# Attention products as three 16-bit products, with another order of the stages in a step

## The reference, cut to what matters

```python
qkv = silu(hidden_states @ qkv_w.T)            # q, k, v of 32 heads x 64
# blocks of 32 tokens, a running state per head:
aw = einsum('bhid,bhjd->bhij', qi, ki) * dd    # dd: decay by distance, 0 above the diagonal
intra = einsum('bhij,bhjd->bhid', aw, vi)
inter = einsum('bhid,bhde->bhie', qi * qd, state)
new_state = state * bd + einsum('bhsd,bhse->bhde', ki * kd, vi)
attn = rmsnorm(intra + inter) * norm_w
gate = sigmoid(hidden_states @ gate_w.T)
x = layernorm(hidden_states + gate * attn @ out_w.T)
x = layernorm(x + moe(x))                      # grouped top-6 of 64 experts, and a shared one
```

## Time and profile before

| | |
|---|---|
| median of 3 timed runs | 1415.9 us (1414.46 to 1415.93) |
| the profiled execution | 1412.41 us, span 1410.4 us |
| mean granted TensorE clock | 0.981 of full speed |
| busy: TensorE, VectorE, ScalarE, GpSimd | 1345.9, 894.6, 671.2, 366.5 us |

### The profile page before, as it was taken

How to read it: one execution, slowest core, us unless ns; L and a number is a source line. 1 busy time by engine, 2 the same in 40 slices (tenths; PEclk the granted TensorE clock), 3 DMA queues, 4 the chain that set the end, 5 groups by cost and what they waited for, 6 DMA issues and landing times.

```text
span 1410.4 us, 36483 instructions
## 1 busy us (share of the span) xinstructions
PE 1345.9 (95%) x13995; PEld 1096.4 (78%) x13995; DVE 894.6 (63%) x2468; ACT 671.2 (48%) x1290; POOL 366.5 (26%) x422
## 2 busy tenths in 40 slices
PE   7999999999999999999999999999999999989960
PEld 5888888888888888888888888888888888865530
DVE  7856576666667575756576666667575756553337
ACT  8644454545454544445454545444444445433314
POOL 0212121212121122212121212121122222337754
PEclk9999999999999999999999999999999999999985
DMA  8500000000000000000000000000000000779957
GB/s 314 194 9 10 25 15 24 15 24 15 24 15 24 7 17 22 7 26 13 24 15 24 15 24 15 24 15 24 7 14 25 7 24 15 228 247 248 239 111 303
DMA packets 52962, 86.38 MB, mean 61 GB/s; under 512 B 6752, under 2 KB 32192, under 8 KB 52032
## 3 DMA queue, kind: packets, MB, share of 16 engines
q1 hardware_dynamic: 41728, 70.33, 14.7%
q0 software_dynamic: 5632, 8.26, 3.4%
q10 hardware_dynamic: 5568, 7.34, 1.5%
HBM read 60.08 MB, written 25.83 MB: 61 GB/s over the span
## 4 chain that ended last, share of the span: by engine, by line
PE 89%; DMA 4%; DVE 3%; issue 1%; POOL 1%; ACT 1%; SPq 0%; ACTq 0%; DVEq 0%; POOLq 0%
PE pA L467 25%; PE pB L467 23%; PE pC L543 13%; PE pO L557 12%; PE pS L529 10%; DMA sums<-sb_stage,sb_sidx 2%; PE pC L467 1%; PE pS L718 1%; DMA sb_W<-sums 1%; PE pC L577 1%; PE pB L701 1%; POOL sums L1292 0%; PE pS L701 0%; DVE sb_W L921 0%; DMA sb_stage<-gather_rows,sb_gidx 0%
## 5 line engine op out<-in xcount | busy, mean ns | idle before, releaser
L467 PE MATMUL pB<-sb_xh,sb_W 128*128 (+1 forms) x2048 | 349.9, 273 | 0.0
L1244 POOL TENSOR_TENSOR sb_fold<-sb_sq 128x256 f32<-128x256 f32 x128 | 111.5, 871 | 893.9 <-ACT sb_sq L801 893.9
L467 PE MATMUL pB<-sb_xl,sb_W 128*128 (+1 forms) x1024 | 279.3, 273 | 0.0
L467 PEld LDWEIGHTS pB<-sb_xh,sb_W 128*128 128x128 f16 x2048 | 200.5, 98 | 23.8 <-issue 0.2
L799 ACT ACTIVATE sb_yh<-sb_y 128x512 f16<-128x512 f32 x128 | 80.6, 630 | 286.4 <-DVE sb_y L937 286.4
L543 PE MATMUL pC<-sb_S,sb_v 128*64 128x256 f32 (+1 forms) x2048 | 194.7, 332 | 0.0
L945 DVE TENSOR_TENSOR sb_ql<-sb_q,sb_qh 128x512 f16<-128x512 f32 x128 | 88.0, 687 | 167.7 <-ACT sb_qh L775 164.3
L774 ACT ACTIVATE sb_q<-pA 128x512 f32<-128x512 f32 x128 | 76.4, 597 | 223.2 <-PE pA L467 223.1
L467 PE MATMUL pA<-sb_xh,sb_W 128*128 (+1 forms) x1024 | 175.9, 274 | 5.7 <-DVE sb_W L921 5.7
L467 PE MATMUL pA<-sb_W,sb_xh 128*128 128x256 f16 x1024 | 177.0, 275 | 2.1 <-ACT sb_qh L775 2.1
L557 PE MATMUL pO<-sb_Wo,sb_yh 128*128 128x256 f16 x1024 | 174.7, 273 | 1.0 <-DVE sb_yl L941 1.0
(11 more groups left out here) (210 smaller groups left out, 2315.5 us busy)
## 6 DMA issues: line engine op xcount, KB each, us to landing
sb_stage<-wprep SPq DMA_DIRECT2D x7, 1280.0 KB, 6.6
sb_W<-sums SPq DMA_DIRECT2D x16, 512.0 KB, 11.1
sb_W<-w_experts SPq DMA_DIRECT2D x16, 384.0 KB, 5.4
gather_rows<-sb_xr SPq DMA_DIRECT2D x16, 320.0 KB, 2.3
sb_D<-w_experts SPq DMA_DIRECT2D x12, 384.0 KB, 4.4
sb_xs<-xT SPq DMA_DIRECT2D x17, 256.0 KB, 2.9
sb_D<-decay SPq DMA_DIRECT2D x8, 512.0 KB, 7.6
sb_xn<-x SPq DMA_DIRECT2D x16, 256.0 KB, 3.0
```

The costliest lines, as they stand in the source:

```text
L467: last = nc.tensor.matmul(dst, a, m, start=(i == 0), stop=(i == len(terms) - 1), **kw)
L1244: nc.gpsimd.tensor_tensor(fold[:, :], sq[:, 0:T], sq[:, T:2 * T], ALU.add).then_inc(s_fold, 1)
```

## The change

1. **Attention in 16 bit.** v and S get an upper part (vh, Sh) and a lower part (vl, Sl) in 16 bit. `attention` makes three products (vh Sh, vl Sh, vh Sl) where it had one in float32. The upper parts are made on ScalarE (`high_v`, `high_S`), the lower part of v on GpSimd (`low_v`), the lower part of S for the first 256 columns of each head on GpSimd and for the other 128 on VectorE (`low_S`).
2. **Decay product** in two instructions over all four heads, first part then second.
3. **Order.** On TensorE: project_q, scores(g-1), project_k, attention(g-2), project_v, output(g-3), project_gate. The small pieces move: sum of squares to q=2, transposes to the end of q=3, router to q=4, counts to q=6, all but the transposes right behind `scores`. On VectorE `decayed` comes first, then `gate`, low_q, low_k, low_S, low_y, with the routing spread between. On ScalarE the squares come before the upper part of y.
4. **Space and semaphores.** wsh and triu32 lie in xr until they are used; the first three units lie in the weights' staging buffer; the decay tables use two semaphores in place of eight, so the load of a table waits for the one two before it.
5. **Tail.** The units are shared out differently over the tail's steps.

```diff
-        v32 = [sb(f"v32{i}", [P, NT, QH * HD]) for i in range(2)]
+        v32 = sb("v32", [P, NT, QH * HD])
+        vh = [sb(f"vh{i}", [P, NT, QH * HD], F16) for i in range(2)]
+        vl = [sb(f"vl{i}", [P, NT, QH * HD], F16) for i in range(2)]
+        Sh = sb("Sh", [P, QH, T + P], F16)
+        Sl = sb("Sl", [P, QH, T + P], F16)
...
-        TAIL = ["g0 g1", "d0 g2 d1 g3 d2 g4", "", "d3 d4", "g5 g6 d5 g7 d6", "", "g8 d7 g9 d8 g10 d9", "", "g11 d10 d11"]
+        TAIL = ["g0 g1", "d0 g2", "d1 g3 d2 g4", "", "g5 g6 d5 g7 d6", "g8 d7 g9 d8 g10 d9", "", "", "g11 d10 d11"]
+        BETWEEN = "d3 d4"
+        HALVES = [(0, T), (T, T + P)]
...
             def load_decays(Q):
-                sp.dma_start(D[:, Q, :], decay[Q]).then_inc(s_decay[Q], 16)
+                wait(sp, s_decay[Q % 2], 16 * (Q // 2))
+                sp.dma_start(D[:, Q, :], decay[Q]).then_inc(s_decay[Q % 2], 16)
...
             def attention(q, h):
-                pe.wait_ge(s_Sm, 2 * h + 2)
-                pe.wait_ge(s_ve, h + 1)
+                pe.wait_ge(s_Sl0, h + 1)
+                pe.wait_ge(s_Sl1, h + 1)
+                pe.wait_ge(s_vl, h + 1)
                 wait(pe, s_sq, h)
+                wait(pe, s_y, h)
                 i = q % 2
+                products = [(vh[i], Sh), (vl[i], Sh), (vh[i], Sl)]
                 for u in range(2):
-                    for t in range(NT):
-                        for e in range(2):
...
+                    for t, (a, z_) in enumerate(HALVES):
+                        for n, (v, s) in enumerate(products):
+                            for e in range(2):
+                                head = 2 * u + e
+                                last = nc.tensor.matmul(pC[64 * e:64 * e + 64, u * T + t * P:(u + 1) * T],
+                                                        v[:, t, head * HD:(head + 1) * HD], s[:, head, a:z_],
+                                                        start=(t == 0 and n == 0), stop=(t == NT - 1 and n == len(products) - 1))
                 last.then_inc(s_C, 1)
...
                 if has(g):
                     project_q(b, q, g)
-                    project_k(b, q, g)
                 if has(g - 1):
                     scores((q - 1) % NQ, g - 1)
+                if behind(b):
+                    if q == 2:
+                        sum_squares(b, g - 2)
+                    if q == 4:
+                        router(b)
+                    if q == 6:
+                        count(b, g - 2)
+                if has(g):
+                    project_k(b, q, g)
...
                 if has(g - 2):
                     bank_of_attention(b, q)
                     attention((q - 2) % NQ, g - 2)
...
                 if has(g):
                     project_v(b, q, g)
+                if has(g - 3) and not (tail and q == 1):
+                    output(b, (q - 3) % NQ, g - 3)
+                if has(g):
                     project_gate(b, q, g)
-                if has(g - 2):
-                    output(b, (q - 2) % NQ, g - 2)
-                if behind(b):
-                    piece(b, q, g - 1)
...
+                if behind(b) and q == 3:
+                    transpose_rows(b, g - 1)
...
             def act_v(q, g):
                 act.wait_ge(s_v, g + 1)
+                wait(act, s_vl, g)
+                nc.scalar.activation(v32[:, :, :].rearrange("p t n -> p (t n)"), pA[:, :], ACT.Silu,
+                                     scale=1 / W_SCALE).then_inc(s_ve, 1)
+
+            def high_v(q, g):
+                act.wait_ge(s_ve, g + 1)
                 wait(act, s_C, g - 1)
...
+                nc.scalar.activation(vh[q % 2][:, :, :], v32[:, :, :], ACT.Copy).then_inc(s_vh, 1)
+
+            def high_S(h, i):
+                act.wait_ge(s_Sm, 2 * h + i + 1)
+                wait(act, s_C, h)
+                a, z_ = HALVES[i]
+                nc.scalar.activation(Sh[:, :, a:z_], S[:, :, a:z_], ACT.Copy).then_inc(s_Sh, 1)
...
-            def decayed(b, q, h, u):
...
+            def decayed(b, q, h):
+                dve.wait_ge(s_S, 2 * h + 2)
...
+                d = D[:, q, :].rearrange("p (h n) -> p h n", h=QH)
+                wait(dve, s_Sl0, h)
+                nc.vector.tensor_tensor(S[:, :, 0:T], pS[:, :, 0:T], d, ALU.mult).then_inc(s_Sm, 1)
+                wait(dve, s_Sl1, h)
+                nc.vector.tensor_tensor(S[:, :, T:T + P], pS[:, :, T:T + P], d[:, :, 0:P], ALU.mult).then_inc(s_Sm, 1)
+
+            def low_S(h):
+                dve.wait_ge(s_Sh, 2 * h + 2)
+                a, z_ = HALVES[1]
+                nc.vector.tensor_tensor(Sl[:, :, a:z_], S[:, :, a:z_], Sh[:, :, a:z_], ALU.subtract).then_inc(s_Sl1, 1)
...
+            def low_v(q, g):
+                pool.wait_ge(s_vh, g + 1)
+                wait(pool, s_C, g - 1)
+                nc.gpsimd.tensor_tensor(vl[q % 2][:, :, :], v32[:, :, :], vh[q % 2][:, :, :], ALU.subtract).then_inc(s_vl, 1)
+
+            def low_S(h):
+                pool.wait_ge(s_Sh, 2 * h + 1)
+                a, z_ = HALVES[0]
+                nc.gpsimd.tensor_tensor(Sl[:, :, a:z_], S[:, :, a:z_], Sh[:, :, a:z_], ALU.subtract).then_inc(s_Sl0, 1)
```

More of the change, by code:

```diff
@@ new lines, in router, with count @@
+            def router(b):
+                pe.wait_ge(s_x1T, b)
+                for t in range(NT):
+                    last = group(pC[:, t * EXP:(t + 1) * EXP],
+                                 [(x1T[:, c, t * P:(t + 1) * P], wr[:, c, :]) for c in range(NC)])
+                last.then_inc(s_r, 1)
+            def count(b, attended):
+                bank_free(attended)
+                pe.wait_ge(s_mask, b)
+                nc.tensor.matmul(pC[0:EXP, 0:T], mask[:, 0, :], triu[:, 0:T], start=True, stop=False)
+                nc.tensor.matmul(pC[0:EXP, P:T], mask[:, 1, :], triu[:, 0:P], start=False, stop=True).then_inc(s_cum, 1)
@@ L846, in step @@
                     split_weights(q + 1, (0, 1))
+                if behind(b) and q == 4 and not tail:
+                    evacuate_router(b)
                 if has(g):
@@ L967, in residual @@
             def residual(b):
-                chain = Chain(dve, s_ln1, LN1_LINKS * (b - 1), s_dve_passed)
                 dve.wait_ge(s_D, 8 * b)
@@ L1106, in step @@
                     split_weights(q + 1)
+                if has(g - 1):
+                    decayed(b, (q - 1) % NQ, g - 1)
+                if behind(b):
+                    if q == 3:
+                        statistics(b)
+                    if q == 4:
+                        route_scores(b)
+                    if q == 5:
+                        route_experts(b)
+                if has(g - 2):
+                    gate((q - 2) % NQ, g - 2)
                 if has(g):
@@ L1110, in step @@
                     split_weights(q + 1, (0, 1))
+                if behind(b) and q == 3:
+                    normed(b)
                 if has(g):
@@ L1258, in step @@
                 last_b = isinstance(b, int) and b == SEQS
-                if last_b and q == 2:
-                    unit_product(2)
+                if has(g - 1):
+                    low_v((q - 1) % NQ, g - 1)
                 if behind(b) and q == 2:
@@ L1265, in step @@
                         unit_product(3)
+                if behind(b) and q == 3:
                     pool.wait_ge(s_var, b)
                     nc.gpsimd.tensor_tensor(rstd2[:, 0:NT], vv[:, 0:NT], mhalf[:, 0:NT], ALU.pow).then_inc(s_rstd2, 1)
+                if has(g - 1):
+                    low_S(g - 1)
                 if has(g - 2):
```

194 lines of the change are left out of this document (100 added, 94 removed).

## The result

| | before | after |
|---|---|---|
| median | 1415.2 us (1413.3 to 1415.9, 4 runs) | 1493.4 us (1491.4 to 1496.9, 4 runs) |
| span of the profiled execution | 1410.4 | 1493.8 |
| first projection of sequence 1 (read at ScalarE's evacuation of q) | 80.9 | 97.2 |
| mean length of a sequence in the loop | 75.66 | 79.27 |
| from the same evacuation in the last step (127) to the end | 203.9 | 219.0 |

The changed kernel is 5.6% slower (ratio 1.056, 95% interval 1.053 to 1.058), where 1396 was forecast. The table divides the 83 us between the two spans: 16 before sequence 1, 52 from there to step 127, 15 behind it.

The account below looks back on a forecast made before the run. TensorE's own work was taken to bound the loop. Attention -32, the q=2 wait +7.5 and the first sequence +5 gave -19.5 us, median 1415.9 to 1396, range 1380 to 1418.

Parts of the forecast that it names:

- TensorE's part: Attention block in each step: 16-bit products and four change-overs take 1.27 us against 1.54; 0.25 saved, 128 x 0.25 = 32 us.
- GpSimd's durations: GpSimd's added subtractions in each step: low_v 1.15 us, low_S of 1024 elements 2.2; sum about 5.0 of 8.95 us.
- rival (B): GpSimd and the shared access become the bound; gain gone at about 2.55 us for low_S, near 1471 at 3.0; chance 0.17.
- Who would be late: The four engines' orders laid side by side in a step: three tight places, only one priced, 7.5 us in all.
- the sum of squares at q=2: TensorE's sum_squares right behind scores waits for GpSimd's fold and acc: 0.5 us a sequence, 15 x 0.5 = 7.5 us.
- (2): At q=4 VectorE does low_x1 and route_scores before gate and low_k; kl just in time for next scores; taken as nothing.
- (3): At q=3 transpose_rows needs statistics, rstd2 and normed inside the step; about 0.6 us to spare; taken as nothing.
- 7.4 us of exclusive time: VectorE's two-SBUF-input instructions (2.4 us) plus GpSimd's work (5.0), which exclude each other, in a step of 8.95 us.
- The first sequence: Steps 2 to 6, where ScalarE and VectorE also split weights, take 9.2 to 10.5 instead of 8.95: 5 us lost.
- The tail: From the end of the last projection to the sum of squares, 13.5 us before: no change taken, within 1 us.
- rival (A): Nothing is late, GpSimd's instructions slip between VectorE's: -32 to -36 us, 1380 to 1384; chance 0.16.

Follow-up runs that it names:

- the order alone, freed: Changed kernel with attention left in float32 and only the new order kept, two buffers for multiplied scores, TensorE's program written out: 1436.5 us, ratio 1.013 to 1.016.

## Why the prediction was wrong

**TensorE's part** was right for the products. A plain step is 8.97 against the forecast 8.95. The attention products start 0.11 us apart at 256 columns and 0.05 to 0.06 at 128, as they were priced:

```profile
642.74 0.28 PE L559 MATMUL pC<-sb_Sl,sb_vh 128*64 128x256 f16 x2
642.85 0.22 PE L559 MATMUL pC<-sb_Sh,sb_vh 128*64 128x128 f16 x2
642.90 0.22 PE L559 MATMUL pC<-sb_Sh,sb_vl 128*64 128x128 f16 x2
```

With the subtractions left out and no fetches, a sequence takes 73.86: 1.80 less, where 8 x 0.25 = 2.0 was the term. The change-over was 0.11, not 0.09. That run's 1396 is the forecast number by chance: it leaves out work, it has the later unit loads, and it has not the stalls that the forecast held.

**TensorE's part left out the loop's turn.** I counted products and not instructions. The body grew from 1697 to 1828 and began elsewhere, and each turn waits 1.7 to 2.3 us for instructions, at times with a slower clock behind it. The runs put 41 us on it where nothing else is late, 10 in the changed kernel as it stands. No row of before shows a gap, but the profile's page had the queue with its 20 packets, and the trace their times: none between 145.7 and 1219.9 us. That was the sign that the body stayed where it was; that it only just did, no row of before could tell.

**GpSimd's durations** were right: 2.13 us alone (2.2 taken), low_v 1.15. The mean with hold-ups was 2.54. By the layout of rival (B) that would have been the break-even, 1419, and not 1493, so its layout failed as mine did.

**"Who would be late" is the step that failed.** It priced one wait, 0.5 us for the sum of squares at q=2 (7.5 us in all). That wait did not come: in the changed kernel the sum of squares follows the scores without a gap. The two places that it took at nothing, (2) and (3), cost 1.70 us (scores behind `low_k` of q=4) and 0.97 us (transposes behind the norm) in every sequence, 15 x 2.67 = 40 us. Steps 3 and 5 grew from 10.04 and 9.59 to 10.75 and 11.17. The reasons are two. I laid the orders out with each engine's own durations and added up 7.4 us of exclusive time in 8.95, as if the holds would fall into idle time; but an instruction that starts just behind a 2.2 us one stands still for all of it, and its engine's queue with it. And I counted VectorE's four instructions with two SBUF inputs only. The norm's tensor_scalar has one tensor in SBUF, and is held too (1.45 us for 0.41; a pair took 2.88 us in the chain), as are the mask and the penalty of the routing (1.07 for 0.29, 0.91 for 0.18), which lie between the lower parts. Together, taking the subtractions out gives 56 us, first sequence included. The page SBUF — State Buffer of the Trainium skill (two separate sides) has both points: the whole instruction is held, and VectorE's two-port modes take part as well as two SBUF inputs. I had used half of it. The runs agree that the instructions are held; in which mode the norm's ran they don't show, for its 0.41 us is what L958 takes for as many elements.

**The first sequence** was 16 us longer, not 5: the same hold-ups on steps that already held the weight splits. Without the subtractions it is within 0.3 us of before.

**The tail** was taken as nothing and the change lost 15 us there; 8 of them came back with the loads moved (9 us in the timed runs). I followed TensorE's blocks and not SyncE's queue, on which moving `route_weights` to the end of step 7 also moved the loads. The other 7 us stay unexplained; with the order alone, freed, the tail is 15 us longer too, and has the late loads.

The three parts add up: 1493 - 56 - 41 - 9 = 1387, against the 1380 to 1384 of rival (A), nothing late. The first two were measured one after the other (1396.2); that the 9 would come on top is an estimate. So the changed attention products were worth about what the sum said, and the rest was lost outside them. How much of the 56 a kernel that does all the subtractions can keep is open: the best here is 1417.

## What to carry to other kernels

When work moves to GpSimd, price it by what its longest single instruction does to the VectorE instruction that starts right behind it, tensor_scalar included, and cut it into pieces of 128 to 256 elements first (one of 1024 into four: 1493 to 1468; those and the values into pieces of 128: 1431 to 1417). Count the instructions of a loop body and look at the instruction queue of the profile before adding to it: few packets in a long loop mean a body that stays, and a changed offset alone can lose it. Follow each moved step through SyncE's queue as well, to the load that stands behind it.

## What was unexpected in the hardware

- A body of 1697 recorded TensorE instructions cost 2.88 us more a turn after being moved by about 128 instructions, and one of 1769 in the old place cost nothing.
- A gap of about 2 us at the turn was followed, behind 7 of 14 turns in one run, by 3.4 us at half the granted clock.
- Two GpSimd subtractions a step that feed nothing (412 us of busy time) made the kernel 114 us slower, with TensorE, VectorE and ScalarE doing the same work as before.
- Cutting one 1024-element GpSimd subtraction in four raised GpSimd's busy time by 100 us and lowered VectorE's by 120.
